# Eight sequences through four layers: half of a scan's sums move from TensorE to GpSimd

## The reference

```
def step(h, inp):
    xt, dlt, bt, ct = inp
    h = jnp.exp(dlt[:, :, None] * A) * h + (dlt * xt)[:, :, None] * bt[:, None, :]
    return (h, jnp.einsum('bdn,bn->bd', h, ct))
```

```
scores = jnp.einsum('bhqd,bhkd->bhqk', q, k) / jnp.sqrt(jnp.float32(dk))
scores = jnp.where(causal[None, None, :, :], scores, -jnp.inf)
attn = jax.nn.softmax(scores, axis=-1)
out = jnp.einsum('bhqk,bhkd->bhqd', attn, v)
```

## Time and profile before

| | before |
|---|---|
| median of 3 runs | 5371.87 us |
| the profiled execution | 5377.29 us, of it the span 5375.2 us |
| mean granted TensorE clock | 0.931 |
| TensorE / weight loads | 4499.2 us (84%) / 2208.3 us (41%) |
| VectorE / ScalarE / GpSimd | 3330.0 us (62%) / 2666.8 us (50%) / 1911.9 us (36%) |

### The profile page before, as it was taken

One profiled execution on the slowest core, in us unless ns is written; L12 is line 12 of the kernel. 1 busy time (PEld: TensorE's weight loads), 2 busy tenths in 40 slices (PEclk: granted clock), 3 DMA queues, 4 the chain that ended last, 5 costly groups with the idle time before them and its releaser, 6 DMA issues. The chain is left out here.

```text
span 5375.2 us, 70831 instructions
## 1 busy us (share of the span) xinstructions
PE 4499.2 (84%) x22404; PEld 2208.3 (41%) x22502; DVE 3330.0 (62%) x7491; ACT 2666.8 (50%) x4966; POOL 1911.9 (36%) x2206
## 2 busy tenths in 40 slices
PE   4678887988879888898888988798887888889888
PEld 2134334443444434443344433454334443445344
DVE  5766755667556674666655666556765667464445
ACT  2255553556526554365543745445553556436453
POOL 2746520555106541175301852036520555110200
PEclk8889998999989999999989999899998999999789
DMA  3523210332104211042100421023210332101000
GB/s 126 158 72 110 76 53 1 105 96 71 41 3 136 79 61 35 3 161 65 57 28 25 159 63 53 13 67 116 75 50 5 100 99 71 40 3 56 1 28 7
DMA packets 166645, 345.29 MB, mean 64 GB/s; under 512 B 18000, under 2 KB 26704, under 8 KB 166240
## 3 DMA queue, kind: packets, MB, share of 16 engines
q1 hardware_dynamic: 166256, 340.54, 19.9%
HBM read 337.25 MB, written 3.21 MB: 63 GB/s over the span
## 5 line engine op out<-in xcount | busy, mean ns | idle before, releaser
L196 PE MATMUL BANKS<-WB 128*128 128x512 bf16 x1518 | 440.1, 439 | 191.1 <-DVE XN L441 45.0
L1939 ACT ACTIVATE heads_prob<-BANKS 128x512 f32<-128x512 f32 (+3 forms) x768 | 365.3, 519 | 193.3 <-PE BANKS L1834 188.8
L407 POOL TENSOR_TENSOR rstd<-rstd,WF 128x4 f32<-128x4 f32 x48 | 48.5, 1011 | 944.7 <-DVE rstd L428 944.7
L1207 DVE CUSTOM_DVE_ANT_0 attn_biased<-BANKS,attn_toep 128x512 f32<-128x512 f32 x384 | 257.8, 682 | 188.3 <-PE BANKS L1095 134.1
L782 POOL TENSOR_TENSOR heads_work<-heads_work,heads_c_all 128x512 f32<-128x512 f32 x192 | 243.7, 1270 | 293.6 <-DVE heads_work L817 293.0
L196 PEld LDWEIGHTS BANKS<-WB 128*128 128x128 bf16 x1616 | 168.8, 110 | 422.8 <-issue 215.4
L212 POOL TENSOR_TENSOR rstd<-rstd,WF 128x4 f32<-128x4 f32 x24 | 24.3, 1011 | 787.5 <-DVE rstd L230 787.5
L1304 PEld LDWEIGHTS BANKS<-last_x_w,last_x_a 128*128 128x128 f32 x1536 | 214.7, 205 | 175.1 <-ACT last_x_a L1344 91.7
L1977 DVE CUSTOM_DVE_ANT_0 BANKS<-BANKS,WF 128x384 f32<-128x384 f32 (+3 forms) x512 | 241.2, 510 | 70.4 <-PE BANKS L1834 67.8
L1304 PE MATMUL BANKS<-last_x_w,last_x_a 128*128 128x128 f32 x1536 | 222.3, 291 | 71.0 <-ACT last_x_a L1344 71.0
L1980 DVE TENSOR_REDUCE heads_nmax<-BANKS 128x1 f32<-128x512 f32 x384 | 244.2, 682 | 60.1 <-PE BANKS L1834 59.0
(11 more groups left out here) (913 smaller groups left out, 10921.5 us busy)
## 6 DMA issues: line engine op xcount, KB each, us to landing
heads_c_all<-bc_rows SPq DMA_DIRECT2D x192, 256.0 KB, 3.2
attn_toep<-bias_line SPq DMA_DIRECT2D x96, 448.0 KB, 4.6
XNM<-bc_rows SPq DMA_DIRECT2D x112, 256.0 KB, 3.1
XTM<-bc_rows SPq DMA_DIRECT2D x112, 256.0 KB, 3.5
XO<-bc_rows SPq DMA_DIRECT2D x112, 256.0 KB, 3.3
XN<-bc_rows SPq DMA_DIRECT2D x112, 256.0 KB, 3.2
heads_b_all<-bc_rows SPq DMA_DIRECT2D x96, 256.0 KB, 3.6
last_x_w<-in_w SPq DMA_DIRECT2D x48, 512.0 KB, 3.7
```

The lines of the kernel that those rows point to most:

```text
L196: nc.tensor.matmul(bank, ident_b, bc(ident_b[:, 0:1], [P, SEQ]), start=True, stop=True)
L1207: V.tensor_tensor_reduce(biased[:, s % NS_, :], PS[s % NS_], toep[:, h % 4, c:c + SEQ], -1.0, BIG, ALU.add, ALU.min, nmax[:, s:s + 1]).the ...
L1939: nc.scalar.activation(prob[:, i % PR, lo:hi], bank("T", i)[:, lo:hi], ACT.Exp).then_inc(exped, 1)
```

## The change

In the heads stage the scan gets `paired=True` (the scan of stage s0 stays as it was). Then GpSimd, after the product of an odd step, adds the odd step's tile to the even one's, in place, and raises the new semaphore `joined`. TensorE issues a summing matmul at odd steps only, on the even step's buffer, and waits for `joined` and not for `rd`. Waits that counted matmuls count half as many (`EACH = 2`): the VectorE scan's wait for its buffer and `flush`'s. GpSimd's odd drives wait for `joined` and not for `acc`. A line for a first step with a state index other than 0 is taken out; no call reached it.

```
-                if m >= 0:
+                if m >= 0 and m % EACH == EACH - 1:
+                    m -= EACH - 1
                     n = step(m)[2]
                     yield at(s) + 0.45 * STEP
-                    if m == 0 and n:
-                        nc.tensor.matmul(SUM, ident, XM[:, :, :].rearrange("p j d -> p (j d)"), start=True, stop=False)
-                    pe.wait_ge(rd, m + 1)
+                    if paired:
+                        pe.wait_ge(joined, m // 2 + 1)
+                    else:
+                        pe.wait_ge(rd, m + 1)
...
-                    nc.tensor.matmul(SUM, ident, work[:, m % RW, :], start=(n == 0), stop=(n == NS - 1)).then_inc(acc, 1)
+                    nc.tensor.matmul(SUM, ident, work[:, m % RW, :], start=(n == 0), stop=(n == NS - EACH)).then_inc(acc, 1)
...
-                    if s >= RW:
+                    if s >= RW and paired:
+                        pool.wait_ge(joined, (s - RW) // 2 + 1)
+                    elif s >= RW:
                         pool.wait_ge(acc, s - RW + 1)
...
                 nc.gpsimd.tensor_tensor(work[:, m % RW, :], work[:, m % RW, :], c_all[:, m % RC, :], ALU.mult).then_inc(rd, 1)
+                if paired and m % 2:
+                    yield at(m) + 1.1 * STEP
+                    pool.wait_ge(rd, m + 1)
+                    even = work[:, (m - 1) % RW, :]
+                    nc.gpsimd.tensor_tensor(even, even, work[:, m % RW, :], ALU.add).then_inc(joined, 1)
...
-                dve.wait_ge(acc, NS * (q + 1) - first)
+                dve.wait_ge(acc, (NS * (q + 1) - first) // EACH)
...
-                    dve.wait_ge(acc, s - RW + 1)
+                    dve.wait_ge(acc, (s - RW) // EACH + 1)
...
-            streams = [mamba_scan(st, XM, 4.0, 6.78, EARLY)] if scan_next else []
+            streams = [mamba_scan(st, XM, 4.0, 6.78, EARLY, paired=True)] if scan_next else []
```

More of the change, by code:

```diff
@@ L683, in mamba_pre, with mamba_scan @@
         return pieces
-    def mamba_scan(st, dest, START, STEP, first=0):
+    def mamba_scan(st, dest, START, STEP, first=0, paired=False):
         STEPS = 2 * ND * NS - first
@@ L697, in mamba_scan @@
         drv = st.sem("drv_even"), st.sem("drv_odd")
-        yev, emptied, ych, outp = (st.sem(n) for n in ("yev", "emptied", "ych", "outp"))
+        yev, emptied, ych, outp, joined = (st.sem(n) for n in ("yev", "emptied", "ych", "outp", "joined"))
         b_ld, c_ld = ([st.sem(f"{n}_ld{i}") for i in range(k)] for n, k in (("b", RB), ("c", RC)))
+        EACH = 2 if paired else 1
         def decay(m):
```

## The result

The changed kernel takes 5485.18 us (median of 3 runs, 5484.15 to 5491.64) against 5371.87: ratio 1.0217, 95% interval 1.0202 to 1.0232. I had said 5404 us, range 5330 to 5475. The direction was right; the loss is 113 us and not 32, and lies outside the range.

What follows compares the result with a forecast made beforehand. The stage was taken to have no single bound: VectorE, then GpSimd in the first attention, TensorE in the second. Removal -46, additions +28 and clock +50 made +32 us, forecast 5404 us, range 5330 to 5475.

Steps and rivals of the forecast that it cites:

- What bounds the stage: Stage with two attentions: no single bound; VectorE, then GpSimd in the first attention, TensorE in the second.
- What it removes: Both attentions: 16 of 32 summing matmuls a stage go, worth 6.6 us a stage, 46 us over seven.
- What it adds: GpSimd, 16 additions a stage: hidden in the second attention, 4.0 us a stage in the first, 28 us in all.
- B: Theory in the experiments, causal attention: the loss is the additions ahead of the masks; additions alone would give 5450 to 5480 us.
- rival 3: GpSimd becomes the bound of the whole causal attention: every addition there counts, +90 us, 5462 us; chance 0.15.
- The new wait: TensorE's matmul for a pair waits for the addition instead of the product; enough slack, cost 0.
- The clock: TensorE, both attentions: fewer summing matmuls mean 20 us more at half clock a stage, 7.2 us each, 50 us in all.
- The sum: Whole kernel: -46 + 28 + 50 = +32 us, forecast 5404 us.
- 1: TensorE's clock holds, its term is 0: -18 us, 5354 us as a median; chance 0.22.
- 2: The clock holds and GpSimd has room, all additions hidden: -46 us, 5326 us; chance 0.08.
- What would show it: Signs in the changed kernel's table by stage: granted clock shares, GpSimd busy time, waits for masks, attention times, last sequence unchanged.

Runs made afterwards that it cites:

- the quarter: The kernel before without the summing matmul of every fourth step (8 of 32 a stage), nothing added: 5462.12 us, ratio 1.0157.

## Why the prediction was wrong, point by point

- **What bounds the stage**: right as read. The seven stages moved, and of the rest only the last sequence's, by 2 us.
- **What it removes, -46 us**: not contradicted, and less sure than it looks. The kernel without half of the sums has 10.5 us more in the causal attention for 39.4 us more at half clock; at 0.31 that is 12.2, so -1.7 us without the clock (I had -2.1). In the second, -1.4 us with 11.4 us more (3.5): -4.9 (I had -4.5). 7 x 6.6 = 46 us. That it meets the forecast so well hangs on the price: at 0.36 the same subtraction gives 7 x 9.2 = 64 us. The only direct comparison, in the second attention at full clock, shows 1 to 2 us for eight of them, with eight additions and three products beside. How much the removal is worth stays open between these.
- **What it adds, +28 us**: near in size, partly by luck. The additions alone cost 24 us (19 to 30). By half clock they move the causal attention 6.8 us up and the second 3.0 us down, at 0.31 some 8 us in all, a term that I did not have; so 16 us are the additions proper, of it 7 x 1.7 = 12 us in the causal attention, where I had put 28. Two in the last part counting whole was too much. That B, or rival 3, would make the loss is excluded.
- **The new wait, 0**: right.
- **The clock, +50 us**: this is the step that failed. "Half way would be +24 and +5 us. I take +15 and +5, because the summing matmuls that stay should end such a stretch". They don't: half clock rose by 44.2 and 15.3 us, and the stretch above goes over three of them. With 44.2 us the causal attention has gone nearly all of the way to the last sequence's 52 us, with only half of the matmuls gone. The term is 7 x (44.2 + 15.3) x 0.31 = 129 us, an estimate by the measured price; at my 0.36 it would be 150. What was wrong is the 20 us at half clock that I took for 59.5, not the price. Both halves of the step were guesses that no row bore: that the loss is in proportion (the quarter shows that it is not), and that one dense matmul brings the clock back. My bound, 149 us, held; I then left it out of the range.
- **The sum**: the stages show 105 us more; 129 - 46 leaves 22 for the additions in the changed kernel. This is by difference, and each of the other two leans on the price. Alone they cost 16 us without their clock; whether the 6 us between are noise, the price, or additions that cost more at half clock, no run tells.
- **Rivals**: 1 and 2 (the clock holds) are excluded by the granted share of 0.75 to 0.81 in the causal attentions. The rule of the Trainium skill ("TensorE: Matmul & The Clock Gate", "Why this matters for your kernels"), that dense issue keeps the clock up, does not agree with this trace as far as busy time goes: 35.60 of 38 us busy at 1.2 GHz. Free of the clock's own effect on busy time is the comparison of fillers of equal length at equal places: 10.2 us at half clock with 128 rows, 54.8 us with 32.
- **What would show it**: I had 0.85 to 0.92 for the causal attention (0.73 to 0.81 came), GpSimd 66 us (65.5), second attention about 99 us at equal clock (102.2 with 15.3 us more at half clock; 4.7 us of that is the clock, so 97.5; but the row starts 1.8 us late, which makes it 99.3). The last sequence's causal attention, which should have been as before, has 86.02 us.

Open: why the fall is so deep in some stages and not in others of one program, and why a quarter missing is worse than a half in the second attention. My guess is that both depend on where in time the remaining matmuls fall; no run here sets that. That it is the rows of the array that count rests on one kernel with 32 rows against the three with 128.

## What to carry to other kernels

Before taking matmuls off TensorE, look at the granted clock of the same work with and without them; here removing half of the summing ones cost some 129 us of clock and won some 46 (both estimates at 0.31 us per us at half clock; the direct comparison shows less of a gain). When a stretch of the profile shows an engine 90% busy at 0.50, try a few short matmuls of no effect there, bf16, all 128 rows, as few as do: twenty of 0.21 us won 3.3 us a stage, 32 long ones won nothing. And take a bound that the trace gives (no scan at all: 52 us at half clock) seriously as a likely value when nothing shows that the way to it is straight. Last, before two rows of a stage are compared, see what their ends hang on: here the start of one hung on GpSimd's queue, and moved 1.8 us with the additions.

## What the runs showed that I had not expected

- At equal time on TensorE, a zero-weight f32 matmul over 128 rows and 32 columns kept the clock as one of 128x128 did (11.2 and 10.2 us at half clock), and one over 32 rows and 128 columns did not (54.8 us).
- One program runs the same code at different clocks from one sequence to the next: causal attention 87.86, 92.49 and 99.55 us in one execution, 0.31 us per us at half clock. In another stretch of code it was 0.40.
- A stage in which nothing was edited moves from kernel to kernel: the last sequence's causal attention has 79.83, 84.16 and 86.02 us in three kernels, with the granted clock at 0.77, 0.69 and 0.65.
- One summing matmul of 1.06 us less in the 7 us before (4.25 and not 5.22 us busy, no idle time over 1.28 us), and the clock fell and stayed at half for 38 us. This is one stage; no run tests that single matmul.
